# Chunk 0 of a fused token, state-space and MoE kernel goes ahead of the other chunks, and the first normalization moves partly into the loop

## The chip, the cores and the metric

The kernel runs on one core of a Trainium2 chip. The metric is the time of one execution on the device, in microseconds (us). Five engines work side by side: TensorE (PE, matrix products and transposes, writes only to PSUM), VectorE (DVE), ScalarE (ACT), GpSimd (POOL), and the queue of SyncE (SP), which starts nearly all loads. Each engine runs its own instructions strictly in the order in which they are written. An engine waits for another by a semaphore: `eng.wait_ge(S("name"), k)` holds the engine, and everything behind that instruction on it, until the semaphore has been raised k times.

## The reference

The input x is 64 x 64 x 64 x 4, a text input is 64 x 32 x 64. The part of the reference that matters here is its first stage:

```
h = einsum('bijf,hf->bijh', x, W) + b, mean over h        # "tokens": 4 features folded with 4 weights
h = concatenate([h, txt], axis=1)                         # 64 sequences x 96 rows x 64 features
u = layernorm(h) @ Win.T + bin                            # normalized, input product
for l in range(4):                                        # four state-space layers
    y = (causal convolution of u with the kernel of A, B, C) + u @ Dm[l].T
    u = layernorm(gelu(y) + u)
h = h + layernorm(u) @ Wout.T + bout
```

After it come a mixture of experts with 16 experts, a causal attention with 8 heads and a recurrent layer over 96 steps. The diff leaves these untouched.

## The kernel before

The 96 rows are cut into six chunks (0 to 5) of 128 partitions x 512 values. Chunks 0 to 3 come from x, chunks 4 and 5 are text. Each chunk goes through this line:

- **tokens(c)**: ACT writes feature 0 of x times its weight (L734, after the load of the chunk has landed), DVE adds features 1 to 3 (L1064, three instructions, each waiting for the one before).
- **front(c)** on DVE: sum over the features (L1072) and centring (L1074). **squares_0(c)** on ACT (L739). **back(c)** on DVE: sum of the squares (L1081) and a small scaling (L1084). POOL then takes the power -0.5 (L229) and multiplies (L231), in `ln_pool`. This is the normalization of one chunk.
- **normalised(c)** on PE: four transposes (L1609); ACT copies them out (**ssm_x**, L743).
- **win(c)** on PE: the input product (L1619); DVE adds the bias while it evicts (**ssm_in**, L1090).

Beside this, a ladder of matrix powers builds the convolution kernels: **powers(i)**, i = 0 to 6, on PE (L1575, L1578, L1580), each waiting for copies of its predecessor by DVE (**krylov**, L1053 and L1056) and ACT (**power**, L727). **weights_turn** (L1587) transposes the layers' weights, **kernels** (L1594) makes the convolution kernels, which DVE evicts (L1102, L1103).

Then comes the loop over chunks and layers, 24 steps (six chunks x four layers; step n has chunk n mod 6). On PE one turn holds: **toeplitz(n-1)** (convolution, L1652), **feature_major(n)** (four transposes, L1636, which wait for ssm_in(n) of the first layer), **du(n-1)** (L1664), **spread(n-1)** (L1672), and in the first turns also normalised(n+2) and win(n+1). On the other engines a step has: ACT's copies **ssm_uf** (L748) and **ssm_c** (L753), **ssm_gelu** (L758) right after spread, DVE's **ssm_y** (L1145), **ssm_centre** (L1152, L1154), ACT's **ssm_sq** (L764), DVE's **ssm_var** (L1162, L1165), and POOL's **ssm_scale** (power L178, multiply L180).

The order is written out by hand for each engine; no scheduler changes it. Before the loop DVE runs front and back of all six chunks, so that the loop itself holds of the first layer's preparation only ssm_in(3) to ssm_in(5) on DVE, and normalised(3) to normalised(5) with win(2) to win(5) on PE. The loads of the weights for weights_turn (`layer_weights` on SP, eight loads, L468 to L472) are issued between chunk 1 and chunk 2 of x (L479).

Of the kernel before, what the change touches and what calls it, by code (L numbers as in the profile page):

```python
# [18 lines left out]
def early_fusion(nc, x, txt, tok_W, tok_b, Win, bin_, Wout, bout, A, Bm, Cm, Dm,  # L19
# [3 lines left out]
    NB, TX, D, NF = x.shape  # L23
# [13 lines left out]
    NC = NM // CH  # L37
    KC = 4
    NJ = NK // KC
# [8 lines left out]
    NS3 = L * (NK // KC)  # L48
    assert NB == 64 and D == 64 and F == 128 and T % 4 == 0 and NK % KC == 0

    with ExitStack() as ctx:
# [69 lines left out]
        def S(name):  # L121
            if name not in sems:
                sems[name] = sem(name)
            return sems[name]
# [199 lines left out]
        for r in range(NR):  # L324
            for g in range(NB // GA):
                for v in range(1 << r):
                    n = GA >> r
# [74 lines left out]
        def begins(g):  # L402
            return g == 0 or g - 1 in AT
# [57 lines left out]
        def _(sp):  # L461
# [11 lines left out]

            xv = x.rearrange("b (m s) i f -> s b m (i f)", s=2)
            for c in XFOLD:
                if c == 2:
                    layer_weights()
                for s in range(2):
                    sp.dma_start(Xr[64 * s:64 * s + 64, c * CH:(c + 1) * CH, :],  # L479
                                 xv[s, :, c * CH:(c + 1) * CH, :]).then_inc(S("ld_x%d" % c), 16)  # L480
# [236 lines left out]
        def _(act):  # L717
# [6 lines left out]
            def power(i):  # L724
                act.wait_ge(S("p_kry"), i + 1)
                nxt = (Am if i == 0 else (Am2 if i % 2 else Am))
                act.activation(nxt[:, 1, :, :], PS[0:D, 1, 0:L * D].rearrange("p (l m) -> p l m", l=L), ACT.Copy).then_inc(S("p_at"), 1)  # L727
# [4 lines left out]
            def tokens(c):  # L732
                act.wait_ge(S("ld_x%d" % c), 32)
                act.activation(H[:, c * CH:(c + 1) * CH, :].rearrange("p m d -> p (m d)"), xcol(c, 0), ACT.Identity,  # L734
                               bias=wm[:, NF:NF + 1], scale=wm[:, 0:1]).then_inc(S("tok0"), 1)

            def squares_0(c):
                act.wait_ge(S("ln_c"), c + 1)
                act.activation(Y2[:, c * 512:c * 512 + 512], XC[:, c * 512:c * 512 + 512], ACT.Square).then_inc(S("ln_q"), 1)  # L739

            def ssm_x(j):
                act.wait_ge(S("w_tp"), j + 1)
                act.activation(UF[:, j * KC:(j + 1) * KC, :], bank4(4 if j == 0 else 5), ACT.Copy).then_inc(S("w_x"), 1)  # L743

            def ssm_uf(n):
                j = n % NJ
                act.wait_ge(S("s_tp"), n + 1)
                act.activation(UF[:, j * KC:(j + 1) * KC, :], bank4(tp_bank(n)), ACT.Copy).then_inc(S("s_uf"), 1)  # L748
# [12 lines left out]
            def ssm_sq(n):  # L761
                sl = slice(n % NJ * 512, n % NJ * 512 + 512)
                act.wait_ge(S("s_c"), n + 1)
                act.activation(Y2[:, sl], XC[:, sl], ACT.Square).then_inc(S("s_q"), 1)  # L764
# [6 lines left out]
            power(2)  # L771
            tokens(1)
            power(3)
            tokens(2)
            squares_0(0)
            power(4)
            tokens(3)
            power(5)
            squares_0(1)
            power(6)  # L780
            ssm_x(0)
            squares_0(2)
            ssm_x(1)
            squares_0(3)
            ssm_uf(0)
            ssm_x(2)
            squares_0(4)
            ssm_c(0)
            ssm_uf(1)
            squares_0(5)  # L790
            ssm_gelu(0)
            ssm_x(3)
            ssm_c(1)
            ssm_uf(2)
            ssm_x(4)
            for n in range(NS3):
                if n + 1 < NS3:
                    ssm_gelu(n + 1)
                ssm_uf(n + 3)
                if n + 2 < NS3:  # L800
                    ssm_c(n + 2)
                ssm_sq(n)
                if n == 0:
                    ssm_x(5)
            ssm_uf(NS3 + 3)

            def gates_exp(p):
# [190 lines left out]
            for g in range(NSLOT):  # L998
# [7 lines left out]
                n = g - 1 if g - 1 < NPR and not begins(g) else None  # L1006
# [32 lines left out]
        def _(dve):  # L1039
# [9 lines left out]
            def krylov(i):  # L1049
                m = 1 << i  # L1050
                nm = min(m, T - m)
                dve.wait_ge(S("p_kry"), i + 2)
                dve.tensor_copy(Gk[:, :, m:m + nm], PS[0:D, 0, 0:L * nm].rearrange("p (l m) -> p l m", l=L)).then_inc(S("p_gk"), 1)  # L1053
                if i < nsq:
                    nxt = Am2 if (i + 1) % 2 else Am
                    dve.tensor_copy(nxt[:, 0, :, :], PS[0:D, 2, 0:L * D].rearrange("p (l m) -> p l m", l=L)).then_inc(S("p_am"), 1)  # L1056


            def tokens(c, f):
                hc = H[:, c * CH:(c + 1) * CH, :].rearrange("p m d -> p (m d)")  # L1060
                dve.wait_ge(S("tok0"), c + 1)
                if f > 1:
                    dve.wait_ge(S("tokf"), (NF - 1) * c + f - 1)
                dve.scalar_tensor_tensor(hc, xcol(c, f), wm[:, f:f + 1], hc, ALU.mult, ALU.add).then_inc(S("tokf"), 1)  # L1064

            def front(c):
                sc = slice(c * CH, (c + 1) * CH)
                if c in XFOLD:
                    dve.wait_ge(S("tokf"), (NF - 1) * (c + 1))
                else:  # L1070
                    dve.wait_ge(S("ld_txt"), 32)
                dve.tensor_reduce(st[:, 0, sc], H[:, sc, :], AX_X, ALU.add).then_inc(S("ln_s"), 1)  # L1072
                dve.wait_ge(S("ln_s"), c + 1)
                dve.scalar_tensor_tensor(XC[:, c * 512:c * 512 + 512].rearrange("p (a d) -> p a d", d=D),  # L1074
                                         st[:, 0, sc].unsqueeze(2).to_broadcast([128, CH, D]), -1.0 / D, H[:, sc, :],
                                         ALU.mult, ALU.add).then_inc(S("ln_c"), 1)

            def back(c):
                sc = slice(c * CH, (c + 1) * CH)
                dve.wait_ge(S("ln_q"), c + 1)  # L1080
                dve.tensor_reduce(st[:, 2, sc], Y2[:, c * 512:c * 512 + 512].rearrange("p (a d) -> p a d", d=D),  # L1081
                                  AX_X, ALU.add).then_inc(S("ln_v0"), 1)
                dve.wait_ge(S("ln_v0"), c + 1)
                dve.tensor_scalar(st[:, 2, sc], st[:, 2, sc], 1.0 / D, EPS, ALU.mult, ALU.add).then_inc(S("ln_v"), 1)  # L1084
# [9 lines left out]
            def layer_weights():  # L1094
                for h in range(2):
                    dve.wait_ge(S("p_bd"), h + 1)
                    dve.tensor_copy(bdt[:, 3 * h:3 * h + 3, :], PS[:, 6 + h, 0:384].rearrange("p (a c) -> p a c", a=3)).then_inc(S("p_bdt"), 1)
# [6 lines left out]


            krylov(0)
            for f in range(1, NF):
                tokens(0, f)
            krylov(1)
            for f in range(1, NF):  # L1110
                tokens(1, f)
            krylov(2)
            front(0)
            tokens(2, 1)
            tokens(2, 2)
            krylov(3)
            tokens(2, 3)
            back(0)
            front(1)
            krylov(4)  # L1120
            for f in range(1, NF):
                tokens(3, f)
            krylov(5)
            layer_weights()
            dve.wait_ge(S("ld_bd"), 16 * 8)
            back(1)
            front(2)
            krylov(6)
            back(2)
            front(3)  # L1130
            kernels()
            ssm_in(0)
            back(3)
            front(4)
            ssm_in(1)
            back(4)
            front(5)
            ssm_in(2)
            back(5)

            def ssm_y(n):
                j = n % NJ
# [23 lines left out]
                                  ALU.mult, ALU.add).then_inc(S("s_v"), 1)  # L1166

            for n in range(NS3):
                ssm_y(n)
                if n:  # L1170
                    ssm_var(n - 1)
                ssm_centre(n)
                if n < 3:
                    ssm_in(n + 3)
            ssm_var(NS3 - 1)

            def ssm_out(j):
# [374 lines left out]
        def _(pe):  # L1552
# [41 lines left out]
                    last = pe.matmul(PS[:, 3, l * T:l * T + T], BB[:, l, :, :].rearrange("p a b -> p (a b)"), Gk[:, l, :], start=True, stop=True)  # L1594
                last.then_inc(S("p_w"), 1)

            for i in range(5):
                powers(i)
            weights_turn()
            powers(5)  # L1600

            xk = halves(X)
            def normalised(j):
# [94 lines left out]
            pe.wait_ge(S("ii"), 2)  # L1698
            pe.wait_ge(S("one"), 1)
            normalised(0)  # L1700
            powers(6)
            win(0)
            kernels()
            normalised(1)
            for n in range(NS3 + NJ):
                if 1 <= n <= NS3:
                    toeplitz(n - 1)
                if n == NS3 + 4:
                    projections()
                feature_major(n)  # L1710
                if 1 <= n <= NS3:
                    du(n - 1)
                    spread(n - 1)
                elif n:
                    out_product(n - 1 - NS3)
                if n + 2 < NJ:
                    normalised(n + 2)
                if n + 1 < NJ:
                    win(n + 1)


            held = {4: (("s_uf", NS3 + 5),), 5: (("s_uf", NS3 + 6),)}
# [508 lines left out]
```

## Time and profile before

| | |
|---|---|
| median of 3 runs | 752.15 us (748.07 to 757.14) |
| the profiled execution, its own time | 749.54 us |
| its span, first to last instruction | 747.8 us |
| PE busy | 682.9 us, 91% of the span |
| DVE busy | 504.4 us, 67% |
| ACT busy | 371.0 us, 50% |
| POOL busy | 230.9 us, 31% |
| share of the chain that ended last: PE, DVE, ACT | 58%, 22%, 8% |

All times within the span count from its first instruction. The page also gives the span in 40 slices of 18.7 us each. The first slices read:

```profile
PE   5799999889999999888998999979799998999996
PEld 5677876562424223552343443357577776566553
DVE  3868999778565863854587667369777774465644
ACT  2334555425665546544454565536565655333332
POOL 4265899713424040311132102125323422000000
DMA  9951000024223230001331322000000000000000
```

A digit is the busy share of a slice in tenths. The first digit of PE is 5, the second 7: these are the slices (0 to 37 us) in which x comes in and the first chunks are prepared. From the third slice on PE stands at 9. The change lies in the first four slices.

### The profile page before, as it was taken

What the parts mean: (1) busy time and instruction counts of PE and PEld (TensorE: products, weight loads), DVE (VectorE), ACT (ScalarE), POOL (GpSimd) and SP (SyncE); (2) the same over time, 40 slices, a digit from 0 to 9 for tenths busy, and PEclk for the clock granted to TensorE, in tenths of its full rate; (3) what the DMA queues carried; (4) which work ended last, traced back from release to release, by engine and by line L of the source; (5) the groups of instructions that cost most, each with busy time, mean ns of one, the idle gap of its engine ahead of it and who ended that gap; (6) DMA issues with size and microseconds to landing.
All of it is one profiled execution on the core that took longest, in us unless ns stands there. A gap on an engine that the chain in (4) does not pass through costs nothing.

```text
span 747.8 us, 17174 instructions
## 1 busy us (share of the span) xinstructions
PE 682.9 (91%) x6848; PEld 399.8 (53%) x6848; DVE 504.4 (67%) x1118; ACT 371.0 (50%) x721; POOL 230.9 (31%) x215
## 2 busy tenths in 40 slices
PE   5799999889999999888998999979799998999996
PEld 5677876562424223552343443357577776566553
DVE  3868999778565863854587667369777774465644
ACT  2334555425665546544454565536565655333332
POOL 4265899713424040311132102125323422000000
PEclk9999999959999999999999999989999999999999
DMA  9951000024223230001331322000000000000000
GB/s 185 176 81 27 2 3 2 1 72 169 91 99 120 100 119 16 3 30 70 101 100 57 101 85 76 7 1 2 2 2 2 1 2 2 13 11 9 13 11 13
DMA packets 42503, 36.94 MB, mean 49 GB/s; under 512 B 20936, under 2 KB 29944, under 8 KB 42424
## 3 DMA queue, kind: packets, MB, share of 16 engines
q1 hardware_dynamic: 41338, 35.60, 17.8%
q8 instruction: 55, 0.90, 0.5%
q10 hardware_dynamic: 1088, 0.26, 0.2%
q14 instruction: 22, 0.18, 0.1%
HBM read 33.85 MB, written 1.97 MB: 48 GB/s over the span
## 4 chain that ended last, share of the span: by engine, by line
PE 58%; DVE 22%; ACT 8%; issue 6%; DMA 2%; POOL 2%; SPq 1%; DVEq 0%; ACTq 0%; POOLq 0%
PE PS L1916 12%; PE PS L1903 11%; PE PS L1879 5%; PE PS L1951 3%; PE PS L1930 3%; PE PS L2007 2%; PE PS L2018 2%; PE PS L1972 2%; DVE am L1384 2%; PE PS L1865 2%; DVE LS L1474 2%; DVE LS L1487 2%; PE PS L1664 2%; ACT LS L995 1%; PE PS L1672 1%
## 5 line engine op out<-in xcount | busy, mean ns | idle before, releaser
L1916 PE MATMUL PS<-Y,W1f 64*128 64x512 f32 x384 | 110.7, 653 | 4.6 <-ACT XC L874 3.6
L1903 PE MATMUL PS<-XC,w2s 128*64 128x512 f32 x384 | 106.0, 632 | 0.4 <-ACT BIG L865 0.4
L874 ACT ACTIVATE XC<-PS 128x1024 f32<-128x1024 f32 x68 | 69.3, 1022 | 52.2 <-PE PS L1903 49.9
L1345 DVE TENSOR_TENSOR Y<-XD,UF 128x512 f32<-128x512 f32 x96 | 69.9, 733 | 6.1 <-DMA UF<-gd 3.2
L1879 PEld LDWEIGHTS PS<-LS,V 64*64 64x64 f32 x1140 | 40.6, 134 | 51.4 <-DVE LS L1487 47.5
L655 POOL TENSOR_TENSOR st<-st,mhalf 128x8 f32<-128x8 f32 x12 | 21.5, 1795 | 134.3 <-DVE st L1332 134.3
L1879 PE MATMUL PS<-LS,V 64*64 64x32 f32 x1140 | 51.1, 222 | 8.7 <-DVE LS L1487 6.4
L1903 PEld LDWEIGHTS PS<-XC,w2s 128*64 128x64 f32 x384 | 19.4, 137 | 73.6 <-issue 62.0
L1916 PEld LDWEIGHTS PS<-Y,W1f 64*128 64x128 f32 x384 | 30.7, 189 | 44.8 <-issue 27.8
L1474 DVE SCALAR_TENSOR_TENSOR LS<-LS 128x32 f32<-128x32 f32 x96 | 19.5, 203 | 49.7 <-ACT LS L989 26.6
L670 POOL TENSOR_TENSOR st<-st,mhalf 128x8 f32<-128x8 f32 x6 | 10.1, 1689 | 115.4 <-DVE st L1465 115.4
L1813 PE MATMUL PS<-w2s,W1f 128*128 128x288 f32 (+5 forms) x110 | 45.0, 490 | 0.0
L1384 DVE TENSOR_REDUCE am<-PS 128x8 f32<-128x768 f32 (+2 forms) x28 | 29.7, 1060 | 22.1 <-PE PS L1954 19.0
L178 POOL TENSOR_TENSOR st<-st,mhalf 128x8 f32<-128x8 f32 x24 | 40.6, 1691 | 11.1 <-DVE st L1165 10.0
L919 ACT ACTIVATE Y<-PS 96x1024 f32<-96x1024 f32 (+1 forms) x28 | 28.6, 1020 | 29.9 <-PE PS L1972 29.8
L995 ACT ACTIVATE LS<-LS 128x32 f32<-128x32 f32 x96 | 22.0, 229 | 33.2 <-DVE LS L1480 33.1
L989 ACT ACTIVATE LS<-PS 128x64 f32<-128x64 f32 x64 | 14.3, 224 | 45.7 <-PE PS L1879 45.7
L2007 PE MATMUL PS<-Y,UT 32*64 32x128 f32 (+2 forms) x768 | 35.5, 275 | 0.8 <-ACT EX L897 0.8
L687 POOL TENSOR_TENSOR Y<-Y,am 128x768 f32<-128x768 f32 (+1 forms) x10 | 16.4, 1644 | 57.0 <-DVE am L1371 32.8
L1487 DVE SCALAR_TENSOR_TENSOR LS<-LS 128x32 f32<-128x32 f32 x96 | 19.0, 198 | 20.0 <-ACT LS L995 20.0
L1930 PE MATMUL PS<-BIG,MMs 64*128 64x512 f32 x96 | 28.0, 660 | 4.3 <-DVE BIG L1337 1.7
L2007 PEld LDWEIGHTS PS<-Y,UT 32*64 32x64 f32 (+2 forms) x768 | 27.8, 134 | 6.5 <-issue 4.6
(255 smaller groups left out, 1455.8 us busy)
## 6 DMA issues: line engine op xcount, KB each, us to landing
UF<-gd SPq DMA_DIRECT2D x192, 128.0 KB, 2.9
BIG<-in_x SPq DMA_DIRECT2D x8, 512.0 KB, 10.1
out<-X SPq DMA_DIRECT2D x48, 32.0 KB, 2.0
W1f<-in_L_ffn_w SPq DMA_DIRECT2D x2, 512.0 KB, 7.6
EX<-in_L_ffn_w SPq DMA_DIRECT2D x1, 1024.0 KB, 15.5
H<-in_txt SPq DMA_DIRECT2D x2, 256.0 KB, 12.9
w2s<-in_L_ffn_w SPq DMA_DIRECT2D x1, 512.0 KB, 10.6
gd<-EX SPq DMA_DIRECT2D x6, 64.0 KB, 1.5
```

The lines of the kernel that those rows point to most:

```text
L178: pool.tensor_tensor(st[:, 3, sj], st[:, 2, sj], mhalf[:, 0:KC * 2], ALU.pow).then_inc(S("s_r"), 1)
L874: act.activation(Hb[:, b:b + 2, :], PS[:, b:b + 2, :], ACT.Relu).then_inc(S("m_h"), 1)
L1345: dve.tensor_tensor(Rb[:, n % 4, :], XD[:, q * 512:(q + 1) * 512], GB[:, n % NS, :], ALU.mult).then_inc(S("m_x"), 1)
L1384: dve.tensor_reduce(stat_a(u, 0), scores(UNITS[u]), AX_X, ALU.max).then_inc(S("a_mx"), 1)
L1474: dve.scalar_tensor_tensor(Cb[:, 0, :], tb[:, 0:HN], 1.0, tb[:, HN:2 * HN], ALU.add, ALU.mult).then_inc(S("l_a"), 1)
L1487: dve.scalar_tensor_tensor(HB[:, t % 4, :], tb[:, 2 * HN:G3], 1.0, TC, ALU.add, ALU.mult).then_inc(S("l_h"), 1)
L1813: pe.matmul(PS[:, b, 0:n], W1f[:, 0, :], w2s[:, 0:8, :].rearrange("p e d -> p (e d)")[:, 0:n], start=True, stop=True)
L1879: mm = pe.matmul(PS[r, b, o:o + HN], V3[r, g, :], HB[r, (t - 1) % 4, :], start=False, stop=True, skip_group_check=True)
L1903: mm = pe.matmul(PS[64 * h:64 * h + 64, 6, :], w2s[:, 2 * p + h, :], Hb[:, n % 2 * 2 + h, :], start=(p == 0), stop=(p == E // 2 - 1))
L1916: mm = pe.matmul(PS[:, n % 2 * 2 + h, :], W1f[r, 2 * p + h, :], Rb[r, n % 4, :], start=True, stop=True)
L1930: mm = pe.matmul(PS[:, b + h, :], MMs[p, half, :, :].rearrange("p a d -> p (a d)"), XAb[p, b0:b0 + GA, RB * r:RB * r + RB], start=True, st ...
L2007: mm = pe.matmul(PS[64 * a:64 * a + 64, z_bank(JOBS[u] + k), x * 128:(x + 1) * 128], XT[p, u % 2, x, :], PT[p, u % 2, a, x, :], start=True ...
```

## The change

Four orders are rewritten; no computation is added or removed.

- SP: the eight weight loads are issued after chunk 0 of x, ahead of chunk 1 (before: ahead of chunk 2).
- PE: weights_turn stands after powers(2) (before: after powers(4)); normalised(0), win(0) and feature_major(0) stand between powers(4), powers(5), powers(6) and kernels; win(1) stands ahead of the loop. In the loop normalised(n+1) stands between du(n-1) and spread(n-1) (before: normalised(n+2), behind spread(n-1)).
- DVE: the tokens of chunks 2 and 3 are interleaved with the normalization and ssm_in of chunks 0 and 1. front(3) and back(3), front(4) and back(4), front(5) and back(5) now stand in turns 0 to 2 of the loop, behind ssm_y, ssm_var and ssm_centre of the step.
- ACT: squares_0, ssm_x and the copies follow that order; in turns 0 to 2 ssm_x(n+3), ssm_gelu(n+1), squares_0(n+4) and ssm_sq(n) stand ahead of ssm_c(n+2) and ssm_uf(n+3).
- POOL's order is the same.

```diff
             for c in XFOLD:
-                if c == 2:
+                if c == 1:
                     layer_weights()
...
             for n in range(NS3):                      # ACT
+                if 3 <= n + 3 < NJ:
+                    ssm_x(n + 3)
                 if n + 1 < NS3:
                     ssm_gelu(n + 1)
-                ssm_uf(n + 3)
-                if n + 2 < NS3:
+                if 4 <= n + 4 < NC:
+                    squares_0(n + 4)
+                if n < 3:
+                    ssm_sq(n)
                     ssm_c(n + 2)
-                ssm_sq(n)
-                if n == 0:
-                    ssm_x(5)
+                    ssm_uf(n + 3)
+                else:
+                    ssm_uf(n + 3)
+                    if n + 2 < NS3:
+                        ssm_c(n + 2)
+                    ssm_sq(n)
...
             for n in range(NS3):                      # DVE
+                if n == 0:
+                    front(3)
                 ssm_y(n)
                 if n:
                     ssm_var(n - 1)
                 ssm_centre(n)
                 if n < 3:
-                    ssm_in(n + 3)
+                    back(n + 3)
+                if n + 2 < NJ:
+                    ssm_in(n + 2)
+                if n < 2:
+                    front(n + 4)
...
-            for i in range(5):                        # PE
+            for i in range(3):
                 powers(i)
             weights_turn()
-            powers(5)
+            powers(3)
+            powers(4)
...
             normalised(0)
+            powers(5)
+            win(0)
             powers(6)
-            win(0)
+            feature_major(0)
             kernels()
             normalised(1)
-            for n in range(NS3 + NJ):
-                if 1 <= n <= NS3:
+            win(1)
+            for n in range(1, NS3 + NJ):
+                if n <= NS3:
                     toeplitz(n - 1)
...
                 feature_major(n)
-                if 1 <= n <= NS3:
+                if n <= NS3:
                     du(n - 1)
+                    if n + 1 < NJ:
+                        normalised(n + 1)
                     spread(n - 1)
-                elif n:
+                    if n + 1 < NJ:
+                        win(n + 1)
+                else:
                     out_product(n - 1 - NS3)
-                if n + 2 < NJ:
-                    normalised(n + 2)
-                if n + 1 < NJ:
-                    win(n + 1)
```

How the order of DVE changes ahead of the loop can be read from the instructions themselves (line numbers of the changed kernel lie 3 above those of before on DVE, 5 or 6 above on PE). This is DVE of the changed kernel from the first tokens to the weights; L1067 is tokens, L1056 and L1059 krylov, L1075 and L1077 front, L1084 and L1087 back, L1100 the weights:

```order
L1067 SCALAR_TENSOR_TENSOR H<-BIG,wm,H 128x512 [waits tokf,tok0]
L1056 COPY Gk<-PS 64x4x2 [waits p_kry]
L1059 COPY Am<-PS 64x256
L1067 SCALAR_TENSOR_TENSOR H<-BIG,wm,H 128x512 [waits tokf,tok0]
L1075 TENSOR_REDUCE st<-H 128x8 [waits tokf]
L1077 SCALAR_TENSOR_TENSOR XC<-st,H 128x512 [waits ln_s]
L1056 COPY Gk<-PS 64x4x4 [waits p_kry]
L1059 COPY Am<-PS 64x256
L1067 SCALAR_TENSOR_TENSOR H<-BIG,wm,H 128x512 [waits tok0]
L1084 TENSOR_REDUCE st<-Y 128x8 [waits ln_q]
L1087 TENSOR_SCALAR st<-st 128x8 [waits ln_v0]
L1100 COPY bdt<-PS 128x384 [waits p_bd] x2
```

The copies that powers(2) waits for (L1056, L1059 of the first pair) stand behind two of the three tokens of chunk 0, where all three stood before, and the normalization of chunk 0 follows at once.

In the loop, this is one turn of PE before (L1652 toeplitz, L1636 feature_major, L1664 du, L1672 spread, L1609 normalised, L1619 win):

```order
L1652 MATMUL PS<-WB,UF 64x96 x8
L1636 MATMUL PS<-ident,UT 128x128 x4
L1664 MATMUL PS<-bdt,UF 128x64 x8
L1672 MATMUL PS<-Cx,ii 64x256 x4
L1609 MATMUL PS<-ident,X 128x128 x4
L1619 MATMUL PS<-bdt,UF 128x128 x4
```

and this the same turn of the changed kernel (L1658, L1642, L1670, L1615 normalised, L1678 spread, L1625 win):

```order
L1658 MATMUL PS<-WB,UF 64x96 x8
L1642 MATMUL PS<-ident,UT 128x128 x4
L1670 MATMUL PS<-bdt,UF 128x64 x8
L1615 MATMUL PS<-ident,X 128x128 x4
L1678 MATMUL PS<-Cx,ii 64x256 x4
L1625 MATMUL PS<-bdt,UF 128x128 x4
```

The transposes of the next chunk have moved ahead of spread. On DVE, this is the changed kernel from ssm_y(1) (L1144) to ssm_y(2); L1161 and L1164 are ssm_var(0), L1151 and L1153 ssm_centre(1), L1084 and L1087 back(4), L1093 ssm_in(3), L1075 and L1077 front(5):

```order
L1144 TENSOR_TENSOR Y<-Y,UT 128x512 [waits s_gelu]
L1161 TENSOR_REDUCE st<-Y 128x8 [waits s_q]
L1164 TENSOR_SCALAR st<-st,lnab 128x8 [waits s_v0]
L1151 TENSOR_REDUCE st<-Y 128x8 [waits s_y]
L1153 SCALAR_TENSOR_TENSOR XC<-st,Y 128x512 [waits s_s]
L1084 TENSOR_REDUCE st<-Y 128x8 [waits ln_q]
L1087 TENSOR_SCALAR st<-st 128x8 [waits ln_v0]
L1093 TENSOR_TENSOR UT<-PS,binr 128x512 [waits w_mm]
L1075 TENSOR_REDUCE st<-H 128x8 [waits ld_txt]
L1077 SCALAR_TENSOR_TENSOR XC<-st,H 128x512 [waits ln_s]
L1144 TENSOR_TENSOR Y<-Y,UT 128x512 [waits s_gelu]
```

Before, the same stretch held only ssm_y, ssm_var, ssm_centre and one ssm_in; back(4) now stands behind a wait for ssm_gelu(1) (`s_gelu`).

## Rows read from the trace of the kernel before

**Rows 1.** Chain of waits that ended last (start us, us, what), start of the span

```profile
4.57 0.69 SPq L468
...
10.01 0.63 SPq L479
10.67 10.87 DMA BIG<-in_x
```

**Rows 2.** Timeline of PE, 7 to 72 us (start, us, line, tiles, count, idle before)

```profile
10.08 0.98 PE L1575 MATMUL PS<-Gk,Am 64*64 64x2 f32 x8 [0.62 <-DVE Am L1056]
...
29.96 1.06 PE L1575 MATMUL PS<-Gk,Am 64*64 64x32 f32 x8
...
32.72 1.11 PE L1609 MATMUL PS<-ident,X 128*128 128x128 f32 x4
...
34.87 2.06 PE L1619 MATMUL PS<-bdt,UF 128*128 128x128 f32 x8
...
41.55 1.11 PE L1636 MATMUL PS<-ident,UT 128*128 128x128 f32 x4 [1.40 <-DVE UT L1090]
...
46.49 1.11 PE L1664 MATMUL PS<-bdt,UF 64*128 64x64 f32 x16
47.53 1.08 PE L1672 MATMUL PS<-Cx,ii 128*64 128x256 f32 x8
48.55 0.65 PE L1609 MATMUL PS<-ident,X 128*128 128x128 f32 x4
49.04 1.06 PE L1619 MATMUL PS<-bdt,UF 128*128 128x128 f32 x8
...
50.88 0.66 PE L1636 MATMUL PS<-ident,UT 128*128 128x128 f32 x4
...
65.73 0.66 PE L1636 MATMUL PS<-ident,UT 128*128 128x128 f32 x4 [0.51 <-DVE UT L1090]
...
68.79 0.66 PE L1636 MATMUL PS<-ident,UT 128*128 128x128 f32 x4
```

**Rows 3.** Timeline of DVE, 11 to 60 us

```profile
11.19 3.58 DVE L1064 SCALAR_TENSOR_TENSOR H<-BIG,wm,H 128x512 f32<-128x512 f32 x3 [1.21 <-ACT H L734]
...
46.48 0.17 DVE L1084 TENSOR_SCALAR st<-st 128x8 f32<-128x8 f32 x1
...
57.77 0.69 DVE L1162 TENSOR_REDUCE st<-Y 128x8 f32<-128x512 f32 x1 [1.37 <-ACT Y L764]
58.49 0.29 DVE L1165 TENSOR_SCALAR st<-st,lnab 128x8 f32<-128x8 f32 x1
58.69 0.68 DVE L1152 TENSOR_REDUCE st<-Y 128x8 f32<-128x512 f32 x1
59.40 0.69 DVE L1154 SCALAR_TENSOR_TENSOR XC<-st,Y 128x512 f32<-128x512 f32 x1
```

**Rows 4.** Timeline of ACT, 14 to 58 us

```profile
14.79 1.29 ACT L734 ACTIVATE H<-BIG,wm 128x512 f32<-128x512 f32 x1 [1.50 <-DMA BIG<-in_x]
...
48.66 0.60 ACT L758 ACTIVATE Y<-PS 128x512 f32<-128x512 f32 x1
...
54.21 0.60 ACT L743 ACTIVATE UF<-PS 128x512 f32<-128x512 f32 x1 [2.04 <-PE PS L1609]
54.71 0.59 ACT L758 ACTIVATE Y<-PS 128x512 f32<-128x512 f32 x1
...
57.10 0.63 ACT L764 ACTIVATE Y<-XC 128x512 f32<-128x512 f32 x1
```

**Rows 5.** Timeline of POOL, 46 to 50 us

```profile
46.73 1.64 POOL L229 TENSOR_TENSOR st<-st,mhalf 128x8 f32<-128x8 f32 x1 [1.61 <-DVE st L1084]
48.45 1.04 POOL L231 TENSOR_TENSOR X<-XC,st 128x512 f32<-128x512 f32 x1
```

**Rows 6.** Windows of PE (stretch: us, busy, count, granted clock, DMA share, GB/s)

```profile
144.00:147.00 3.00, 2.08 (x10) 1.00 0.00 0
148.00:151.00 3.00, 2.69 (x13) 0.50 0.00 0
```

## What the change should do to the time

> **What bounds the kernel now.** I read the slices of the page first: PE is the engine that fills the span, and only its first two slices leave room. Then the chain of waits through the first 70 us. It starts on SP, passes the eight weight loads (from 4.57 to the next load of x at 10.01, so 5.4 us of SP) and then hangs on chunk 2 of x, which lands at 10.67 + 10.87 = 21.5 [rows 1]. After that it runs over DVE, and feature_major(0), the first piece of the loop, starts only at 41.55 [rows 2], behind ssm_in(0).
>
> Inside the loop I read when feature_major starts: 50.88 for step 2, 65.73 for step 5, 68.79 for step 6 [rows 2]. So steps 2 to 5, in which chunks are still being prepared, take 14.85 / 3 = 4.95 us each, and the next takes 3.06, with PE busy throughout. Everything behind step 6 is an unbroken row of such steps, whose order the change leaves alone, and no load is due there later than before. So the whole question is **when feature_major(6) starts**: 68.79 now, and any shift of it is a shift of the end.
>
> TensorE's clock matters too. The same four transposes last 1.11 us at 32.72 and at 41.55 and 0.65 to 0.66 from 48.55 on; the eight passes of win last 2.06 at 34.87 and 1.06 at 49.04 [rows 2]. So it ran at its 1.2 GHz level up to some point between 41.55 and 46.49, and at 2.4 GHz after it.
>
> **The start, part by part.** Durations of one stage from rows at the lower clock level:
> - DVE does one of three tokens in 3.58 / 3 = 1.19 [rows 3]. With krylov(1) behind two of them, its two copies end near 11.19 + 2.4 + 0.5 = 14.1, where powers(2) begins.
> - One powers(i) takes 32.72 - 29.96 = 2.76 [rows 2], so it ends at 16.8. weights_turn, six transposes at 1.11 / 4, adds about 1.6: 18.4. Its loads are now ahead of chunk 1, so they have landed. powers(3) ends at 21.1, 0.6 goes to copies between (as the idle ahead of the row at 10.08) [rows 2], powers(4) ends at 24.4.
> - normalised(0) about 0.9, powers(5) 2.8, win(0) 2.0, powers(6) 1.0: feature_major(0) starts at about **31**, against 41.55. That is a lead of 10.6 us. Chunk 0's last token ends near 15.3; its back(0) stands behind one token of chunk 1 (landed 16.6, see below; ACT 1.3, DVE 1.2) and ends near 20, and POOL's 2.8 [rows 5] bring 22.8, before PE asks at 24.4.
> - kernels (2.0 at most, by win's row of the same number of passes) and normalised(1) end at 35.1, the copy 0.6, win(1) and toeplitz(0): together 50.88 - 49.04 = 1.84 at the upper level, at the lower one times 2.06 / 1.06, so 3.5. feature_major(1) starts at 39.2 to 39.3, du adds 47.53 - 46.49 = 1.04, normalised(2) 0.5, so spread(0) starts at 41.3 at the upper level [rows 2].
> - The moved loads: chunk 1 of x, taken at 14.79 before [rows 4], can be as much as 5.4 us later if the queue is dry meanwhile, and 0 if the loads only change places. SP's issue is what moves; 1.8 us (the time of eight small loads within a busy queue, read from where chunk 2 lands) is my estimate. Chunk 1's tokens are wanted by DVE only from 17.4 on, so it costs nothing up to 2.5 us, and chunk 2 lands where it did.
>
> **The loop.** Here a ring of waits appears that the kernel before doesn't have. normalised(k+1) on PE waits for POOL's multiply of chunk k+1; that for back(k+1) on DVE; that stands behind ssm_y(k-2), which waits for ssm_gelu(k-2), and that for spread(k-2), which on PE stands behind normalised(k). So **each normalization waits for the one before it, once around four engines**. Around the ring:
> - normalised to spread 49.04 - 48.55 = 0.49, spread to gelu 48.66 - 47.53 = 1.13 [rows 2, 4]
> - gelu, then squares_0 and ssm_sq on ACT, which issues 0.50 apart, to ssm_var: 0.50 + 0.50 + 0.63 + 0.04 = 1.67 [rows 4]. ssm_y runs beside it.
> - ssm_var 0.72 and 0.20, ssm_centre 0.71 and 0.69, back 0.72 (same form as L1162) and 0.25 to POOL [rows 3, 5]
> - power 48.45 - 46.73 = 1.72, multiply 1.04 and 0.05 to PE: 2.81 [rows 5]
>
> Sum: **9.4 us a turn**, against 4.95 now. Before, the two halves (back of all chunks, and the steps) ran side by side.
>
> It goes: gelu(0) at 41.3 + 1.13 = 42.5, ssm_y 43.1, ssm_centre 0.72 + 0.71, back(3) 0.69 + 0.72, 0.25, POOL 2.81: normalised(3) at about 49.0. Two turns of the ring: normalised(4) at 58.4, normalised(5) at 67.8. Then spread(3) 68.3, gelu 69.4, ssm_y and ssm_var 1.3 later, ssm_centre and ssm_in(5) to 73.1, its 0.7, feature_major(5) at 73.9 against 65.73, and 3.06 later feature_major(6) at 76.9 against 68.79. **The lead of 10.6 us turns into a loss of 8.1 us**, with TensorE at its upper level from 39 on. Nothing is charged in it for hand-overs that collide.
>
> **The clock.** Before, matmuls stood without a break through the first steps and the clock was up by 46.49. In the ring PE has per turn 0.6 (feature_major) + 1.0 (du) + 0.5 + 1.0 (spread) + 1.8 (win, toeplitz) = 5.0 us of work [rows 2] and idles 4.4, most of it in one piece. What follows such idling the trace shows once: with PE busy 2.08 of 3 us from 144 to 147, the granted clock was 0.50, its 1.2 GHz level, in the stretch from 148 [rows 6]. The Trainium skill, "TensorE: Matmul & The Clock Gate", section "HAM oscillation — how this bites in real kernels", says of loops whose bursts of matmuls are parted by waits that the clock drops again in each wait and every burst starts cold; by that rule all turns would be at the lower level, which is the rival below. From rows: a turn at the lower level costs 0.46 more for normalised and, by the ratio 2.06 / 1.06, 1.1 more for spread [rows 2], so 10.9. The start to spread(0) costs about 2.3 more at the lower level (du, spread's end, the transposes), and a PE-bound step behind the ring 3.06 x 0.94 = 2.9 more, until the clock rises. I take half the start (1.2), one of the two turns (1.5) and a third of a step (1.0): 3.7.
>
> **Sum:** 8.1 + 3.7 = 11.8. On the profiled execution, 749.54, that is 761.3. The median of the runs shown is 752.15, 2.6 above it, and gives 763.9. I take **762**.
>
> **Rivals**
> - **Upper level throughout.** The ring alone, 8.1: 757.6 on the profiled time. It holds if PE may idle 4.4 us in each of two or three turns and keep its clock; the row of 144 to 147, with 0.9 of 3 us idle, speaks against it. Chance 0.2.
> - **Lower level throughout the ring and beyond.** 8.1 + 2.3 + two turns 3.0 + two steps 5.8 = 19.2: 769. Against it: the start has its matmuls without a break from 24 to 43 us, as long a dense stretch as the one in which the clock rose before. Chance 0.13.
> - **Not slower: the lead carries through the loop.** If normalised(3) to normalised(5) find their multiply done, steps keep their 4.95 and feature_major(6) comes at 46.7 + 14.85 + 3.06 = 64.7, where 46.7 is feature_major(2) behind ssm_in(2) (45.9): a gain of 4.1, 745.4. With the whole lead of 10.6 kept, 739. Its place is normalised(4), and it decides by whether POOL's multiply ends within 4.95 us of the previous one. No term of the ring can shrink that far: POOL's and DVE's parts alone are 2.81 + 3.3. Chance 0.08.
> - **The weight loads hold chunk 1 back.** Up to 5.4 us late; then tokens(1), front(1) and with them normalised(1) slide by the 2.9 us beyond the slack, on top of the forecast: 765. Chance 0.07.
>
> The forecast has 0.52. Its own range is 757 to 766.
>
> **Range and chances.** The three runs shown lie 9 us apart, for which I have no row, so I take the medians to compare to some 3 us. 755 to 769 takes in the ring at either clock level and leaves out the kept lead and the far ends: about 2 in 10. A measurement of this kernel can tell about 1% from no change, 7.5 us. The gaining rival gives faster 0.04 and same 0.04; the upper level lies at the border and gives half to same (0.1), the forecast gives 0.1 to same; the rest is slower.
>
> **What would show it.** After: feature_major(0) near 31; feature_major(2) near 47; then steps of 9 to 11 us with PE idle for about 4 us at feature_major, waiting for ssm_in, and a short wait of normalised for POOL's L231; feature_major(6) at 77 to 82; ssm_y waiting over 3 us for gelu in turns 1 to 3. Granted clock below 1 somewhere between 45 and 80. From step 7 on rows as before. I am wrong if steps 2 to 5 stay near 5 us, or if the loss arises behind step 6.

## The result: slower by 2.0%, and more than was forecast

| | before | changed |
|---|---|---|
| median of 5 runs each | 755.82 us (748.07 to 758.75) | 770.86 us (765.28 to 780.57) |
| profiled execution, its own time | 749.54 us | 770.86 us |
| span | 747.8 us | 769.1 us |

The ratio is 1.020, 95% interval [1.014, 1.027]; here and below a ratio leaves out runs over 1.5% above the fastest of their kernel, here 778.7 and 780.6. The direction was forecast, the size was not: 762 was predicted, 755 to 769 was the range. Between the two medians lie 15.0 us, between the two profiled executions 21.3; the first is the result, the second is what the traces below explain.

The first slices of the page after, to be held against those of before (18.7 us a slice then, 19.2 now):

```profile
PE   6977899888999999897998999989899998999996
PEclk9996699985999999999999999989999999999999
```

PE, which stood at 9 from the third slice on, now has 7 and 8 in slices 3 to 5, and the granted clock is 0.6 in slices 4 and 5. The page prints 9 for slices 1 and 2 too, though the trace's first record of the clock stands at 46.0 us: as [rows 2] show by their durations, the engine runs at its 1.2 GHz level in them.

The timeline of PE after, the rows of feature_major (L1642, the row L1636 in [rows 2]) for steps 0, 2 to 8:

```profile
31.22 1.11 PE L1642 MATMUL PS<-ident,UT 128*128 128x128 f32 x4
...
49.87 0.66 PE L1642 MATMUL PS<-ident,UT 128*128 128x128 f32 x4 [2.28 <-DVE UT L1093]
...
59.28 0.84 PE L1642 MATMUL PS<-ident,UT 128*128 128x128 f32 x4 [3.79 <-DVE UT L1093]
...
70.46 1.12 PE L1642 MATMUL PS<-ident,UT 128*128 128x128 f32 x4 [3.08 <-DVE UT L1093]
...
81.52 1.12 PE L1642 MATMUL PS<-ident,UT 128*128 128x128 f32 x4 [3.27 <-DVE UT L1093]
...
87.14 1.12 PE L1642 MATMUL PS<-ident,UT 128*128 128x128 f32 x4
...
93.28 0.86 PE L1642 MATMUL PS<-ident,UT 128*128 128x128 f32 x4
...
96.68 0.66 PE L1642 MATMUL PS<-ident,UT 128*128 128x128 f32 x4
```

Step 0 starts 10.3 us earlier than before (41.55), step 2 still 1.0 earlier, step 5 at 81.52 instead of 65.73, step 6 at 87.14 instead of 68.79, step 8 at 96.68 instead of 75.28. That last difference, 21.4 us, is that of the spans, 769.1 - 747.8 = 21.3: behind step 8 nothing more is lost. The durations in the second column tell the clock: 1.11 is the 1.2 GHz level, 0.66 the 2.4 GHz level.

The windows of PE after (stretch: us, busy, count, granted clock, DMA share, GB/s):

```profile
46.00:58.00 12.00, 6.66 (x80) 1.00 0.31 56
60.00:66.00 6.00, 6.00 (x34) 0.50 0.10 21
81.00:93.00 12.00, 11.48 (x88) 0.50 0.01 1
```

From 46 to 58 PE is busy little more than half the time, still at full clock. Then the granted clock falls three times, for 59.6 to 66.4, 69.9 to 76.7 and 80.1 to 93.7, and is back at 1 between them. From 81 to 93 PE is busy 11.48 of 12 us, and the clock stays at the lower level all the same.

The chain of waits after, one turn of the ring (start, us, what):

```profile
63.06 1.93 PE PS L1678 x8
65.02 0.60 ACT Y L758
65.61 0.52 ACT Y L739
66.13 0.53 ACT Y L764
66.68 0.70 DVE st L1161
67.40 0.29 DVE st L1164
67.69 0.60 DVE st L1151
68.32 0.69 DVE XC L1153
69.01 0.61 DVE st L1084
69.64 0.17 DVE st L1087
69.81 0.60 DVE UT L1093
...
70.46 1.12 PE PS L1642 x4
71.57 1.91 PE PS L1670 x16
73.48 1.04 PE PS L1615 x4
74.52 1.93 PE PS L1678 x8
```

spread (L1678), gelu and two squares, ssm_var, ssm_centre, back, and then ssm_in (L1093), feature_major, du (L1670), normalised (L1615), spread again: 11.46 us. It's nearly the ring of the prediction, except for its last third: here it isn't closed by POOL, but by ssm_in and PE. One turn earlier the chain does pass POOL (L229 and L231, 49.30 to 52.07).

### The profile page after: what moved, and what is told of

Its sections match the earlier page's. It is cut to its first block, busy times and chain, and to the rows that moved or that the text cites. A ratio compares the mean times of both kernels' runs of the same rounds, so it can differ in the third digit from the quotient of the medians.

```text
span 769.1 us, 17174 instructions
## 1 busy us (share of the span) xinstructions
PE 698.7 (91%) x6848; PEld 410.1 (53%) x6848; DVE 504.8 (66%) x1118; ACT 371.4 (48%) x721; POOL 231.1 (30%) x215
## 3 DMA queue, kind: packets, MB, share of 16 engines
q1 hardware_dynamic: 41338, 35.60, 17.1%
## 4 chain that ended last, share of the span: by engine, by line
PE 61%; DVE 21%; ACT 8%; issue 6%; POOL 2%; DMA 1%; ACTq 0%; SPq 0%; DVEq 0%; POOLq 0%
PE PS L1925 11%; PE PS L1912 11%; PE PS L1888 5%; PE PS L1960 3%; PE PS L1939 3%; PE PS L2016 2%; PE PS L1678 2%; PE PS L1670 2%; PE PS L2027 2%; PE PS L1981 2%; DVE am L1389 2%; PE PS L1874 2%; DVE XC L1153 2%; DVE LS L1479 2%; DVE LS L1492 2%
## 5 line engine op out<-in xcount | busy, mean ns | idle before, releaser
L1912 PEld LDWEIGHTS PS<-XC,w2s 128*64 128x64 f32 x384 | 19.4, 137 | 73.5 <-issue 61.8
L1479 DVE SCALAR_TENSOR_TENSOR LS<-LS 128x32 f32<-128x32 f32 x96 | 19.5, 203 | 49.7 <-ACT LS L992 26.6
L670 POOL TENSOR_TENSOR st<-st,mhalf 128x8 f32<-128x8 f32 x6 | 10.1, 1690 | 115.4 <-DVE st L1470 115.4
L1642 PE MATMUL PS<-ident,UT 128*128 128x128 f32 x120 | 22.4, 315 | 15.7 <-DVE UT L1093 12.4
L748 ACT ACTIVATE UF<-PS 128x512 f32<-128x512 f32 x30 | 17.9, 597 | 37.3 <-PE PS L1642 37.3
L1144 DVE TENSOR_TENSOR Y<-Y,UT 128x512 f32<-128x512 f32 x24 | 19.1, 798 | 24.9 <-ACT Y L758 24.9
```

Source lines behind the costliest of these rows:

```text
L1479: dve.scalar_tensor_tensor(Cb[:, 0, :], tb[:, 0:HN], 1.0, tb[:, HN:2 * HN], ALU.add, ALU.mult).then_inc(S("l_a"), 1)
L1912: mm = pe.matmul(PS[64 * h:64 * h + 64, 6, :], w2s[:, 2 * p + h, :], Hb[:, n % 2 * 2 + h, :], start=(p == 0), stop=(p == E // 2 - 1))
```

## The experiments

**The clock held up.** 20 transposes ahead of feature_major(2) to (5) keep PE busy while it waits.

```diff
+                if 2 <= n <= 5:
+                    filler(n, 20)        # 20 transposes into bank 4, which feature_major overwrites
                 feature_major(n)
```

> The changed kernel with 20 extra transposes on PE ahead of feature_major(n) for n = 2 to 5, where PE idled 2.3, 3.8, 3.1 and 3.3 us. They write a PSUM bank that feature_major overwrites; no result depends on them. At the upper clock level 20 of them take about 3 us (the trace has four in 0.6), less than the idle piece they stand in. Theory C (the clock): the ring alone costs 8 us and TensorE's lower level the other 13 of the 21 us by which the profiled end moved. Then the clock stays up, the turns go back from 9.8 and 11.5 us to 9.2 to 9.6, feature_major(8), at 96.7 in the changed kernel and 75.3 before, starts at 83 to 87, and the span falls by 9 to 13 us to 756 to 760. Rival R (the ring alone, or load on PE): the extra work changes nothing or delays, feature_major(8) stays at 96 or later and the span at 769.

Measured: median 768.27 us over 4 runs beside 751.71 over 7 of before, ratio 1.024 [1.017, 1.032]. feature_major (here L1646) and normalised (L1615) in its timeline of PE:

```profile
52.17 0.66 PE L1615 MATMUL PS<-ident,X 128*128 128x128 f32 x4 [0.55 <-POOL X L231]
...
61.56 0.65 PE L1615 MATMUL PS<-ident,X 128*128 128x128 f32 x4 [0.55 <-POOL X L231]
...
70.97 0.66 PE L1615 MATMUL PS<-ident,X 128*128 128x128 f32 x4 [0.55 <-POOL X L231]
...
86.63 0.66 PE L1646 MATMUL PS<-ident,UT 128*128 128x128 f32 x4
```

In the stage, theory C holds. Every duration is that of the 2.4 GHz level, the turns are 9.39 and 9.41 us, each closed by POOL, and step 8 starts at 86.63 instead of 96.68: 10.1 us from the clock alone, 11.3 left of the 21.4. But the span did not fall: it is 769.2 us beside the 769.1 of the changed kernel. Counted by the same instruction of DVE from the end, the lag against before is 11.3 us up to 227 us, 16.2 at 259, 14.6 at 488 and 21.3 at 536. The windows of before and of this run over the same work (all engines; the granted clock is the third number from the right):

```profile
227.00:259.00 32.00, 32.00 (x150) 11.61 (x148) 20.94 (x40) 18.96 (x22) 6.00 (x4) 1.00 0.31 102
488.00:536.00 48.00, 41.05 (x557) 30.46 (x558) 39.20 (x51) 24.18 (x27) 19.88 (x12) 0.93 0.01 2
```

```profile
238.00:275.00 37.00, 37.00 (x150) 13.78 (x146) 21.10 (x41) 18.94 (x22) 6.31 (x5) 0.86 0.26 85
502.00:557.00 55.00, 48.59 (x554) 36.26 (x555) 39.37 (x50) 24.45 (x28) 19.87 (x12) 0.78 0.01 2
```

The counts agree but for a few records, the clock does not. Two more experiments asked whether that belongs to the filling.

**Before, a second trace.** The same program as before.

> The kernel before once more, for a second trace of the same program. The run with the filling transposes had its stage 10 us shorter than the changed kernel's, and lost as much in later stages, in stretches at the lower clock that the two first traces don't have. If these stretches fall at random, this second trace differs from the first one in the later stages by several us with a first stage equal within 1 us (feature_major(8) near 75). If they belong to the filling, it doesn't: all stages agree within 1 us.

Measured: 751.70 us, span 750.0. Step 8 starts at 76.26, 1.0 later than in the first trace; by the same count from the end this lag grows by 1.6 between 227 and 259 us and by 2.5 between 488 and 536, shrinks by 1.6 before the one and by 1.6 between them, and is 2.2 at the end. So the late stretches vary with the same program, though here by less than in the filled run. The runs of before, 746.0 to 760.1 in one group of 23, spread by 14 us, more than the two stages of the filled run lost.

**Changed and filled once more, side by side.**

> The changed kernel once more, on the chip and in the rounds of the run with filling transposes. Ring and clock are expected as in the first trace: steps 2 to 5 at 9 to 12 us with stretches at the lower clock, feature_major(8) 17 to 23 us later than in the kernel before, and everything behind it shifted by the same, but for the stretches at the lower clock in later stages, which move the end by 0 to 12 us in either kernel. Median 1.5 to 3% above before.

> The filling transposes once more. If the clock in the loop is worth 10 us as the first pair of traces says, this kernel's median lies 6 to 12 us (0.8 to 1.6%) below that of the changed kernel in the same rounds, and its trace has turns of 9.4 us at the upper level with feature_major(8) near 86.6. If the median is within 2 us of the changed kernel's, the 10 us come back in later stages by something that belongs to the filling, or the filling holds the clock in some executions only; then the trace should show turns at the lower level or the same two late stretches (near 250 and 506) again.

Measured: changed 772.13 us (6 runs, 762.23 to 780.19), filled 763.41 (6 runs, 758.48 to 770.01), before 752.97 (11 runs). The ratios, 1.015 [1.009, 1.021] and 1.016 [1.010, 1.021], show no difference between the two. The medians lie 8.7 us apart, but only because three of the six changed runs took 775 to 780 us; the other three, 762.23, 762.62 and 768.76, lie among the filled ones. So the filling's gain is shown in the stage, by two pairs of traces, and not in the time of the whole kernel. In the traces, step 8 starts at 94.69 in the changed kernel and at 84.44 in the filled one (75.28 and 76.26 before); this time the filled one keeps its lag of 9.2 to the end (8.9), and it is the changed one that loses 6.7 more between 488 and 536, with 20.5 us at the lower level there. The late stretches are not the filling's.

**The two rings.** First only the normalizations of chunks 3 to 5 back ahead of the loop:

```diff
             tokens(3, 3)                          # DVE
+            front(3)
+            front(4)
+            back(3)
+            front(5)
+            back(4)
+            back(5)
...
                 ssm_centre(n)
-                if n < 3:
-                    back(n + 3)
                 if n + 2 < NJ:
                     ssm_in(n + 2)
-                if n < 2:
-                    front(n + 4)
```

with squares_0(3) to (5) ahead of ssm_c(0) on ACT.

> The changed kernel with front(3), back(3), front(4), back(4), front(5), back(5) and their squares ahead of the loop again (DVE and ACT only); ssm_in(n+2) stays behind ssm_y, ssm_var and ssm_centre of turn n, and PE's order stays. Theory P (the ring of my prediction: normalised(k+1) waits for POOL, that for back(k+1) behind ssm_y(k-2), that for spread(k-2) behind normalised(k)): this opens it, steps 3 to 5 fall to about 5 us, feature_major(6) starts at 68 to 70 and the time is that of before within 1%. Theory I (a second ring, through ssm_in: feature_major(k) waits for ssm_in(k) behind ssm_y(k-2), that for spread(k-2), which stands behind feature_major(k-1) and du): it stays closed, steps 3 to 5 still take 7.5 us at the upper clock level and 10.3 at the lower, feature_major(6) starts at 77 to 90 and the kernel stays slower than before by 8 us or more.

Measured: 768.52 us, ratio 1.025 [1.017, 1.032]. Its feature_major(2) to (5):

```profile
53.55 0.66 PE L1642 MATMUL PS<-ident,UT 128*128 128x128 f32 x4 [1.58 <-DVE UT L1093]
...
63.01 0.66 PE L1642 MATMUL PS<-ident,UT 128*128 128x128 f32 x4 [1.35 <-DVE UT L1093]
...
71.83 1.11 PE L1642 MATMUL PS<-ident,UT 128*128 128x128 f32 x4 [2.26 <-DVE UT L1093]
...
82.05 1.11 PE L1642 MATMUL PS<-ident,UT 128*128 128x128 f32 x4 [2.26 <-DVE UT L1093]
```

Steps of 9.5, 8.8 and 10.2 us: theory P alone is refuted. With the ring through POOL open, the one through ssm_in is left: the chain of this run goes from spread over gelu, ssm_y, ssm_var, ssm_centre and ssm_in (62.35) to feature_major (63.01), du, normalised and spread again, in every turn. The 7.5 us expected for it at the upper level can't be held against these turns, since each has part of its work on PE at the lower level (spread takes 1.93 us in each of them).

Then only ssm_in ahead of ssm_y:

```diff
+                if n + 2 < NJ:
+                    ssm_in(n + 2)
                 ssm_y(n)
...
                     back(n + 3)
-                if n + 2 < NJ:
-                    ssm_in(n + 2)
```

> The changed kernel with only ssm_in(n+2) moved from behind ssm_centre and back to ahead of ssm_y(n). Theory P: nothing changes, the normalization's ring stays closed; steps 9.4 to 9.8 us at the upper level and about 12 at the lower, feature_major(6) at 75 to 90, the time that of the changed kernel within 1%. Theory I: ssm_in's ring is the one that sets the pace, so steps fall to about 5 us and feature_major(6) to about 68. If both rings are there, neither this run nor the one with only the backs moved gains much, and only both moves together do.

Measured: 766.44 us, ratio 1.022 [1.016, 1.028]. feature_major(2) to (5):

```profile
45.80 0.66 PE L1642 MATMUL PS<-ident,UT 128*128 128x128 f32 x4
...
56.85 0.66 PE L1642 MATMUL PS<-ident,UT 128*128 128x128 f32 x4 [0.17 <-DVE UT L1093]
...
69.24 0.66 PE L1642 MATMUL PS<-ident,UT 128*128 128x128 f32 x4
...
80.86 0.66 PE L1642 MATMUL PS<-ident,UT 128*128 128x128 f32 x4 [0.20 <-DVE UT L1093]
```

Steps of 11.1, 12.4 and 11.6 us, now with PE's idle time elsewhere. Theory I alone is refuted too. But the edit did more than open the ring through ssm_in, as the chain of this run shows (start, us, what):

```profile
63.32 1.11 PE PS L1615 x4
64.44 1.91 PE PS L1678 x8
66.34 2.02 PE PS L1625 x8
68.38 0.69 DVE UT L1093
```

ssm_in (L1093), now ahead of ssm_y, waits for win (L1625), which on PE stands behind normalised and spread. From ssm_y (69.08) the chain goes on over ssm_var, ssm_centre, back and POOL to the next normalised at 75.60: the ring through POOL with win and ssm_in in the place of gelu, 12.3 us a turn.

Both edits together:

> Both moves of the two other runs in the changed kernel: front and back of chunks 3 to 5 ahead of the loop and ssm_in(n+2) ahead of ssm_y(n). PE's and SP's orders are those of the changed kernel, normalised still ahead of spread. With both rings open steps 3 to 5 take about 4.9 us, PE-bound as before the change; feature_major(2) starts later than in the changed kernel (about 50 against 49.9), feature_major(6) at 67 to 69, and the time is that of before within 1%. If the loss came from PE's order or from the moved loads, it stays at 10 to 20 us over before.

Measured: 757.61 us, ratio 1.011 [1.004, 1.018]. feature_major(2) to (5):

```profile
53.11 0.86 PE L1642 MATMUL PS<-ident,UT 128*128 128x128 f32 x4
...
58.49 0.66 PE L1642 MATMUL PS<-ident,UT 128*128 128x128 f32 x4 [0.17 <-DVE UT L1093]
...
63.66 0.66 PE L1642 MATMUL PS<-ident,UT 128*128 128x128 f32 x4 [0.18 <-DVE UT L1093]
...
68.82 0.65 PE L1642 MATMUL PS<-ident,UT 128*128 128x128 f32 x4 [0.20 <-DVE UT L1093]
```

Steps of 5.2 us, and step 6 at 71.9, 3.1 behind before. Of the 18.4 us that the changed kernel was behind at that step in its first trace, 15.3 are gone with only DVE's and ACT's orders touched. Both rings are real, and either alone is enough. The forecast of "before within 1%" was missed by little: step 2 comes 3 us later than expected, since spread(0) waits 5.53 us for ACT's ssm_c(0), which the edit put behind three squares.

**PE's order undone.**

```diff
                     du(n - 1)
-                    if n + 1 < NJ:
-                        normalised(n + 1)
                     spread(n - 1)
+                    if n + 1 < NJ:
+                        normalised(n + 1)
```

> The changed kernel with normalised(n+1) behind spread(n-1) again on PE; all else as changed. By my prediction's ring, which runs through normalised ahead of spread, this cuts PE's normalised out of the way to ssm_gelu and should give turns of about 8.9 us at most and a gain of 1 to 2 us. By the ring through ssm_in (feature_major(k) waits for ssm_in(k) behind ssm_y(k-2), that for spread(k-2), and spread(k-1) stands behind feature_major(k)), the order of these two is nearly free: steps 2 to 5 stay at 9 to 12 us, feature_major(6) at 77 to 91, the time that of the changed kernel within 1%. If PE's order were the cause of the loss, steps would fall to about 5 us.

Measured: 779.38 us (4 runs, 766.05 to 781.02, too far apart for a ratio). Steps 2 to 5 start at 47.87, 57.13, 69.07 and 80.13, steps of 9.3 to 11.9 us, with the granted clock at 0.5 from 57 to 91. The order of these two on PE is not the cause. Nor does the edit take normalised out of the ring, which was expected of it: ACT's order still has ssm_x, which waits for normalised, ahead of ssm_gelu, and the chain of this run goes from normalised (50.58) over ssm_x (51.20) to gelu (51.80).

**The loads alone.**

```diff
-                if c == 2:
+                if c == 1:
                     layer_weights()
```

> The kernel before with only the eight weight loads issued ahead of chunk 1 of x instead of chunk 2. Chunk 1 should reach ACT at about 16.3 instead of 14.8 (as in the changed kernel), chunk 2 at 21.3 as before. DVE starts the tokens of chunk 1 1.5 us later, has 1 to 2 us of slack there, and feature_major(0) stays within 0.5 us of 41.55; the time is that of before within 0.5%. Rival: the loads' move costs in itself, feature_major(0) 1.5 us later and the time 1 to 2 us up.

Measured: 752.96 us over 10 runs, ratio 1.002 [0.996, 1.007]. ACT takes chunk 1 at 16.49 instead of 14.79 [rows 4], feature_major(0) starts at 41.70 instead of 41.55. Step 6 starts at 69.73, as in the second trace of before (69.77). The moved loads cost nothing that these runs can tell.

**A third order.** Same instructions, all orders of the first 70 us rewritten so that nothing waits in a ring. DVE from kernels on, before the steps turn regular:

```diff
+            kernels(); back(3); ssm_in(1); front(4); front(5); ssm_in(2); back(4)
+            ssm_y(0); back(5); ssm_in(3); ssm_centre(0); ssm_in(4); ssm_var(0)
+            ssm_y(1); ssm_in(5); ssm_centre(1)
```

PE runs normalised(2) to (5) each one or two steps ahead of its feature_major.

> A third order with the same instructions: loads and start as in the changed kernel, but on DVE the normalizations of chunks 2 to 5 spread so that each ends at least a step before it is wanted, ssm_in(n) two steps ahead, normalised(2) ahead of feature_major(1). Both rings are open and the lead of the start is kept in part. From the durations in the traces I expect feature_major(6) at 60 to 64 instead of 68.8 and a stage that ends 5 to 8 us earlier than before; the time 1% below before if the later stages keep their times, 0 to 1% if the clock in later stages takes part of it back. Rival: DVE bounds the start whatever the order, and it ends where before does, feature_major(6) at 67 to 69.

Measured: 755.22 us over 12 runs beside 751.49 over 23, ratio 1.001 [0.996, 1.006]: no difference. In its trace step 6 starts at 61.24 and step 8 at 68.21, 7.1 us ahead of before. But the span is only 3.0 shorter. The waits of ACT's ssm_sq for DVE's centring, from about step 7 to the end of the loop, in this kernel and in before (us in total, times, longest):

```profile
ACT Y L764 <- DVE XC L1204: 18.5, 14, 2.2
```

```profile
ACT Y L764 <- DVE XC L1154: 5.4, 10, 1.1
```

PE got further ahead than DVE: counted by the same instruction of DVE from the end, DVE leads before by 4.4 us at 88 us of before and by 1.5 at 100. There the chain of waits of before itself runs over DVE, from 95 us on over ssm_var, ssm_centre and ssm_sq, 3.5 us a step. A lead of PE beyond DVE's pace is given back. The other 1.5 of the 3.0 us come between 200 and 226 us of before, where its trace has 3.4 us at the lower clock and this one none.

**The late stretch.** 12 transposes ahead of each of the first two groups of gate products, in before and in the third order.

```diff
+                if c < 2:
+                    ...                  # 12 transposes into the bank that the gate products overwrite
                 pe.wait_ge(S("en_h"), 2 * c + 2)
```

> The kernel before with 12 extra transposes on PE ahead of each of the two first groups of gate products (L1748), where PE waited 1.76 us for ACT at 146.6 and after which every trace shows 17 to 24 us at the lower clock (147.3 to 167.8 in the first). They write the bank that the gate products overwrite. If the clock there falls because PE idles, the stretch at the lower clock shrinks or goes, the pieces at 151.8, 153.8, 155.8 and 164.9 take half their time, and the time falls by 3 to 7 us (0.4 to 0.9%). Rival: the gate products of 16 columns don't hold the clock themselves, the stretch stays, and the extra transposes at the lower level cost 1 to 3 us.

> The searched order (both rings open, its trace 3.0 us shorter than the first of before) together with the 24 late transposes. If both effects hold they add: 6 to 10 us below before (0.8 to 1.3%), the fastest version of this study. If the late transposes don't raise the clock, it equals the searched order, within 0.5% of before.

Measured: 754.31 us, ratio 0.998 [0.994, 1.002], and 754.66, ratio 1.002 [0.997, 1.007]. The stretch at the lower clock around 150 us went from 20.5 us to 17.1 in both traces, and no time came of it: the gains of 3 to 7 and of 6 to 10 us that were expected did not come. No version here beats the kernel before.

## Why the prediction was right in its direction and short in its size

- **The start** was right: feature_major(0) near 31 (31.22), feature_major(1) at 39.64 (39.2 to 39.3 said), chunk 1 of x at 16.30 (16.6 taken), the copies for powers(2) done by 14.0. The moved loads cost nothing, as said.
- **The ring** was right, and so was its price at the upper level: 9.4 us a turn said, 9.39 and 9.41 measured with the clock held. From normalised(5) to feature_major(5) 6.1 was said and 6.10 measured there.
- **It was one ring of two.** The prediction says the loop waits "once around four engines", through POOL. A second one, through ssm_in and feature_major, is shorter at the upper level (by the 0.55 us for which normalised still waits for POOL in the filled kernel, so about 8.8 a turn) and hides behind it. At the lower level du (1.91 instead of 1.04), normalised and spread make it the longer one: 11.46 a turn, where "a turn at the lower level ... 10.9" was said. This matters little for the time and much for a cure, since mending either alone mends nothing.
- **The step that failed is the term for the clock**, a term of the right kind that was sized far too small. "I take half the start (1.2), one of the two turns (1.5) and a third of a step (1.0): 3.7." In the first trace it was 13.3 (21.4 - 8.1), by parts: 3.1 before normalised(3) (52.12 instead of 49.0), 0.4 and 2.1 in the two turns, 2.0 up to step 5, 2.6 and 2.8 in the steps 5 to 6 and 6 to 7, 0.2 in the last. The share in steps 5 to 7 was the worst taken: I let the clock rise after a third of a step of dense work, and it stayed low through 11.5 busy us. The filled kernel shows how much of this is the clock in the loop: 10.1 us in the first pair of traces and 10.3 in the second. In the second trace of the changed kernel the whole is 11.3 (19.4 - 8.1).
- **How far the number missed is partly chance.** The sum was a loss of 11.8 us; between the medians it is 15.0, between the profiled executions 21.3. The median of before was 752.15 over three runs when the forecast was made and is 755.82 over five, 3.7 higher. And of the five changed runs 765.28 and 765.43 lie within 755 to 769, the median at 770.86 is 1.9 above it. The term for the clock, 3.7, was short by 9.6 us in the first trace and by 7.6 in the second; that is no chance.
- **The rival "lower level throughout"**, with 19.2 us and a chance of 0.13, came nearest the 21.3 of the first profiled pair. Against it I argued that the clock would be raised by the dense start, and it was, at 46.0; the ring then let it fall again at 59.6. The Trainium skill, "TensorE: Matmul & The Clock Gate", section "HAM oscillation — how this bites in real kernels", says that waits between bursts of matmuls bring the clock down again and again. The trace agrees in the main: 6.66 us busy of 12, then 0.50, three times up to 93.7. Not every burst starts at the lower level, though: normalised(3), behind waits of 2.28 and 0.55 us, takes 0.66 at 52.12.
- **"Everything behind step 6 is an unbroken row"** held for a loss, which went to the end undiminished (21.4 at step 8, 21.3 at the end). It would not have held for a gain, as the third order shows. So the rival "the lead carries through", with its gain of 4.1, was probably priced too high as well.
- **The spread** of 3 us between medians was a little too small a guess: the groups of before have medians from 751.49 to 756.08, and single runs from 746.0 to 760.1. Where two traces of one program differ behind step 8, they do so in stretches at the lower clock, 6.7 us between 488 and 536 in one of the changed kernel. Why these come in one execution and not in the next is open; no experiment here steered them.

## What to carry to other kernels

Before work is moved into a loop, walk every path from an instruction of one turn to the same instruction of the next, over all engines, and add up each path at both clock levels. Moving work from ahead of the loop to behind an instruction that waits for the loop's own product turns two streams that ran side by side into one ring; here two such rings were closed by one edit, and opening either alone gave next to nothing. When PE waits in each turn, price the whole stage at the lower clock level, together with the steps behind it; and a lead of PE is worth only what the next engine in the chain can follow.

## What was not expected of the hardware

TensorE stayed at its lower level from 81 to 93 us though it was busy for 11.48 of 12 us, and in the second trace of the changed kernel from 81 to 91 though it was busy for all 10. The same program takes between 746.0 and 760.1 us, and in two traces of the changed kernel the stage around 510 us alone differs by 6.9 us, with 6.8 us at the lower level in one and 20.5 in the other.
